# Attention loop of a transformer block on eight cores: a TensorE wait after each group of 512 queries is placed three score tiles later

## The reference

```python
def attn(inputs, Wq, Wk, Wv, Wo, rel_emb):
    q, k, v = (split_heads(inputs @ W) for W in (Wq, Wk, Wv))
    position_bias = compute_bias(rel_emb, qlen, qlen)      # by buckets of key position - query position
    scores = jnp.einsum('bnqd,bnkd->bnqk', q, k) + position_bias
    attn = jax.nn.softmax(scores, axis=-1)
    hidden = jnp.einsum('bnqk,bnkd->bnqd', attn, v)
    return merge_heads(hidden) @ Wo

x = x + attn(layernorm(x), Wq, Wk, Wv, Wo, rel_emb)
x = x + ffn(layernorm(x), w1, w2)      # two linear layers with quantised inputs and weights, GELU between
```

## Time and profile before

| | us |
|---|---|
| median of 2 runs | 9241.44 (9235.77 to 9247.11) |
| the profiled execution's own time | 9240.33 |
| its span on the slowest core (core 5) | 9238.8 |
| spans of the other cores | 9213.0 to 9233.7 |
| TensorE busy, core 5 | 3234.0 (35%) |
| ScalarE busy, core 5 | 2029.9 (22%) |
| VectorE busy, core 5 | 2173.7 (24%) |

### The profile page before, as it was taken

The page is one execution under the profiler, slowest core; times in us unless marked ns, Lnnn a source line. Parts: engine busy times, 40 slices in busy tenths (PEclk is TensorE's granted clock), DMA queues, the critical chain, the costliest instruction groups (busy, mean ns, idle before and its releaser), DMA issues.

```text
span 9238.8 us, 47072 instructions; the slowest of 8 cores (9213.0 to 9238.8 us)
## 1 busy us (share of the span) xinstructions
PE 3234.0 (35%) x12444; PEld 1099.6 (12%) x12444; DVE 2173.7 (24%) x2480; ACT 2029.9 (22%) x2214; POOL 85.1 (1%) x164
## 2 busy tenths in 40 slices
PE   0000015667665100133225235676774000233155
PEld 0000001222121000011112011221221000111022
DVE  0334310000000156266600200000001265366400
ACT  0010102545443000022200003454551000122100
POOL 0000000000000000000000000000000000000000
PEclk9999997888787555566667667887886555666577
DMA  3323222000001310200032122000002401200122
GB/s 69 117 94 115 75 59 50 14 27 14 16 25 47 113 40 29 60 23 23 26 89 73 62 54 41 23 14 19 23 14 65 116 27 39 47 23 23 50 76 74
DMA packets 661832, 459.49 MB, mean 50 GB/s; under 512 B 546242, under 2 KB 579140, under 8 KB 653380
## 3 DMA queue, kind: packets, MB, share of 16 engines
q1 hardware_dynamic: 652868, 447.81, 16.9%
q0 software_dynamic: 8704, 8.66, 0.7%
HBM read 209.23 MB, written 143.79 MB: 38 GB/s over the span
## 4 chain that ended last, share of the span: by engine, by line
DMA 21%; PE 20%; DVE 19%; ACT 15%; SPq 12%; issue 7%; DVEq 5%; ACTq 2%; PEldq 0%; PEld 0%; POOL 0%; POOLq 0%
SPq L103 9%; ACT AR L718 6%; PE PS L967 5%; DMA ARF<-w_in 4%; DVEq L276 3%; PE PS L656 3%; DVE qst_b L290 3%; PE PS L699 2%; PE PS L707 2%; DVE qst_u L298 2%; DVE qst_c L285 2%; SPq L106 2%; PE PS L711 2%; ACT qst_t L930 2%; DVE AR L312 2%
## 5 line engine op out<-in xcount | busy, mean ns | idle before, releaser
L893 PE MATMUL PS<-AR 128*128 128x512 bf16 x2016 | 509.4, 420 | 2427.8 <-DMA AR<-xq_dram 1555.0
L718 ACT ACTIVATE AR<-PS,neg40c 128x1024 bf16<-128x1024 f32 x1024 | 1140.2, 1113 | 485.1 <-PE PS L711 310.6
L967 PE MATMUL PS<-AR 128*128 128x512 bf16 x1984 | 458.8, 391 | 725.7 <-DMA AR<-hq_dram 665.0
L766 DVE RECIPROCAL ARF<-ARF 128x32 f32<-128x32 f32 x16 | 5.7, 353 | 2894.7 <-DMA ARF<-ARF 2894.7
L893 PEld LDWEIGHTS PS<-AR 128*128 128x128 bf16 x2016 | 211.3, 106 | 2726.1 <-issue 2535.6
L699 PE MATMUL PS<-AR 64*128 64x512 bf16 x1024 | 435.9, 426 | 246.5 <-ACTq L92 124.3
L604 PE MATMUL PS<-AR 128*128 128x512 bf16 x448 | 135.7, 454 | 973.3 <-DMA AR<-wv_bf 908.4
L707 PE MATMUL PS<-AR,j_sb 128*128 128x512 bf16 x1024 | 439.8, 429 | 0.0
L703 PE MATMUL PS<-AR 64*128 64x512 bf16 x1024 | 437.0, 427 | 0.0
L711 PE MATMUL PS<-AR,j_sb 128*128 128x512 bf16 x1024 | 434.3, 424 | 0.0
L727 PE MATMUL PS<-AR 128*65 128x512 bf16 x1024 | 400.2, 391 | 90.8 <-ACTq L92 90.8
(11 more groups left out here) (111 smaller groups left out, 3552.4 us busy)
## 6 DMA issues: line engine op xcount, KB each, us to landing
ARF<-w_in SPq DMA_DIRECT2D x64, 512.0 KB
ARF<-w_in SPq DMA_DIRECT2D x32, 1024.0 KB
xtile<-x_in SPq DMA_DIRECT2D x64, 512.0 KB
hq_dram<-AR SPq DMA_DIRECT2D x32, 1024.0 KB
AR<-g_dram SPq DMA_DIRECT2D x32, 992.0 KB
x_dram<-x1t SPq DMA_DIRECT2D x32, 512.0 KB
xtile<-x_dram SPq DMA_DIRECT2D x32, 512.0 KB
xtile<-x_dram SPq DMA_DIRECT2D x64, 256.0 KB
```

The source lines that it names most:

```text
L718: E("scalar", lambda S, ewg=ewg, j=j: S.activation(out=ewg[:, 0:1024], in_=PS[:, 1024 * j:1024 * (j + 1)], func=AF.Exp, bias=neg40c[:], sc ...
L893: E("tensor", lambda T, tt=tt, dc=dc, hg=hg: T.matmul(ps[hg], xqT[dc][:, 128 * tt:128 * (tt + 1)], w1qT[dc][:, 512 * hg:512 * (hg + 1)], s ...
L967: T.matmul(ps[bk], hqT[hc][:, 128 * ttl:128 * (ttl + 1)], w2qT[hc][:, 512 * dg:512 * (dg + 1)], start=(hc == 0), stop=False))
```

## The change

TensorE no longer waits for the four copies directly behind the last PV matmul of a group. The count is kept in `pv_guard`, and TensorE waits for it in the next group of the same pair, ahead of the first PV matmul (`pkt == 0`, which is at `kt == 2`), which writes banks 6 and 7 anew. `pv_guard` is set to None at the start of each pair, so the wait behind a pair's fourth group falls away. POOL's wait is unchanged. Nothing that is computed changes.

```diff
@@ -679,6 +679,7 @@
                 sc_hist = {}
                 vv_hist = {}
                 pv_hist = {}
+                pv_guard = None
                 dminus_, dplus_ = _sat_range()
@@ -723,6 +724,8 @@
                         if kt >= 2:
                             pkt = kt - 2
                             ewp = ew[pkt % 3]
+                            if pkt == 0 and pv_guard is not None:
+                                r.wait("tensor", "S", pv_guard)
                             r.wait("tensor", "S", sc_hist[(qg, pkt)])
                             E("tensor", lambda T, hp=hp, pkt=pkt, ewp=ewp: T.matmul(
                                 PS[0:65, 3072:3584],
@@ -749,7 +752,7 @@
                     sc_hist[(qg, NT - 1)] = sc
                     sc_hist[(qg, NT - 2)] = sc
                     sc_hist[(qg, NT - 3)] = sc
-                    r.wait("tensor", "S", sc)
+                    pv_guard = sc
                     r.wait("gpsimd", "S", sc)
                     if qg == 0:
                         r.wait("gpsimd", "V", r.val("V"))
```

## The result

The changed kernel takes 9143.73 us (median of 7 runs, 9126.8 to 9158.54), the kernel before in the same comparison 9239.14 (6 runs, 9235.73 to 9253.45). The ratio is 0.9892, with a 95% interval from 0.988 to 0.9904: 1.1% less, thus within the 2% that was counted as no change, and clear of the noise. The forecast was 9138 us.

A forecast was written before the change was run, and what follows sets the result against it. No one engine bounds the whole kernel; ScalarE bounds the attention loop at 2.4 GHz. 78 + 30 - 5 = 103 us against 9240.3 gave 9137, and 9138 for the median; range 9108 to 9186.

The forecast's parts named there:

- First term: At 48 group boundaries the first exponential starts at 1576.35, not 1577.98: 1.63 us each, 78 us gained.
- Second term: Behind the boundaries the clock stays at 2.4 GHz and 30 us of exponentials' slips go; bounds -5 to +30 us.
- Third term: Projection groups between pairs: shifted starts make two or three stretches longer, 5 us lost, bounds 24 us to either side.
- What was put at nothing: New wait ahead of the first PV matmul, dropped wait at 16 pair ends, copies beside matmuls: no effect each.
- Signs: In the trace: idle time before exponentials falls from 503 to about 395 us, attention clock slices rise by nearly one.
- A: Clock falls at the boundary as before: gain about 68 to 73 us, time 9170; chance 0.18.
- B: Clock falls later, inside the group, after the 1.4 us hole: 2.4 us late per boundary, time 9253; chance 0.03.

## Why the prediction was right

The forecast was 9138, measured 9143.73; the gain was 95 us where the sum said 103. The slowest cores' spans, 96.6 us apart, show it by terms: 78 + 28 - 13, and 3.7 less in other stages, which the sum didn't have.

*First term, 78 us.* Right: the idle time ahead of the first exponential fell from 87.8 us for 48 boundaries to 9.8 in the mean over cores, 78.0 less. It ends at 0.20 and not at 0.25 us, which is nothing. The run with one early tile shows that the term needs only one tile.

*Second term, 30 us, with the clock.* Right in kind and size. The slips fell from 34 to 8 us (26 less in the mean over cores, 28 on the slowest ones), and the clock fell at none of the 48 boundaries, where it had fallen at all 48. The hole is 1.32 us (forecast 1.4), and TensorE is busy for 2.53 of 3.30 us (forecast 2.3). The run with useless matmuls shows that the cause is TensorE's work in the hole, since nothing else was changed there; the runs with one and two tiles show that the amount counts: with 1.05 of 3.30 us busy the clock fell every time, with 1.67 of 3.40 at three boundaries of four, with 2.5 of 3.30 at none. The Trainium skill says that small idle spells between matmul groups can be enough to bring the clock down ("TensorE: Matmul & The Clock Gate", "A second HAM failure mode: psum-queue depth-cycling"). By that rule only the first term, 78 us, would have come. The trace of the changed kernel doesn't agree: holes of 0.78, 0.77 and 1.32 us in a row left the clock at 1.00. The runs with one tile and with the pipelined order and ScalarE's copy agree in most of their boundaries, with holes of 1.74 and 2.50 us.

*Third term, 5 us lost in the projections.* The mean over the cores is 4.7 us lost between the pairs, of it 3.8 in the projections. The longer projections are those in which the clock was at 0.50 for longer. Before, 89 of the 112 took 22.6 us (3.9 of them at 0.50) and 23 took 24.4 (7.9 at 0.50); after, 80 took 22.6, 21 took 24.3, and 11 took 25.9 (12.6 at 0.50), more than the long length of 24.3 that the prediction had. On the two slowest cores 12.7 us are lost (1256 us in the 14 pieces of core 5 before, 1269 on core 3 after, 1245 on the best core after), and of these only 3 lie in the projections: 7.4 are a longer wait for the bias tables behind them, which the prediction took as fixed. Why the tables come later is not shown. These 12.7 in place of 5 are most of the 8 us between sum and measurement.

*What was put at nothing.* The wait ahead of the first PV matmul cost nothing: at the first boundary the copies ended at 1574.97 and exponential 0, for which the same matmul waits, at 1576.28. The pair ends brought nothing (0.9997). The copies stayed at 0.58 us beside matmuls.

*Signs.* The idle time before the exponentials fell to 405.9 and not to 395, since core 3 waits longer for the bias tables. The clock line was to rise by nearly one in each slice of the attention stages; only three slices did, and the granted clock of the whole span went from 0.737 to 0.751.

*Rivals.* A did not occur. B did not occur here, but its mechanism is real: it appears with one early tile (slips of 0.8 us at a boundary, more than the 0.6 of before) and in full with the pipelined order and ScalarE's copy. I had put 2.4 us late, and written that it decides from 2.25 us of slip per boundary on; there two steps behind the copy took 1.39 and 0.35 us too long, 1.7 at that boundary. So even there B's price was too high.

## What to carry to other kernels

When TensorE waits for an engine that still has copies to make, look for work that needs only what is already free: here the score tiles' own banks were free, and only the PV banks were not, so the wait belonged ahead of the first writer of those banks. Price such a hole twice, as late work and as a possible fall of the clock for the work behind it, and check where that work stands: where the clock fell, it cost 0.3 us with three tiles in hand (one ScalarE copy), 1.0 with one early tile, and 1.7 when the next tile stood behind the wait itself (pipelined order with ScalarE's copy). Once the hole was closed, the copies on the bounding engine were the next cost, one for one: one wide copy in place of four narrow ones gave nearly as much (81 us) as the change itself.

## What was not expected

The stages ahead of the attention loop took 1539 to 1559 us up to the first exponential in most programs, but 1557 to 1568 with the useless matmuls and 1594 to 1628 in the three programs in which VectorE makes the copy out of PSUM, though their code up to there is the same and their DMAs move the same bytes (447.8 MB on the hardware queue over the whole span). SyncE's waits for the weight loads, 0 to 1100 us, core 3, of the changed kernel:

```profile
SPq L120 <- DMA ARF<-w_in: 359.3, 96, 6.0
```

and of the version with VectorE's copy:

```profile
SPq L120 <- DMA ARF<-w_in: 396.2, 95, 6.4
```

Each load waits for the one before it, so 0.4 us on each add up to 37 of the 70 us by which the first exponential of this core is later; in one stretch the loads came every 4.2 us in place of 3.4. The waits for other loads of that stage are longer too. It is not the place of the DRAM tensors as far as one shift of 16 MB tells, and it doesn't come with VectorE's copies within SBUF, which the version with one ScalarE copy has too, with the usual start. What it is stays open. The lesson for a comparison: 50 us of a result can lie in a stage that the edit doesn't touch, and a version is judged by its stage in the trace as well as by its total.

One copy of 65 x 1024 out of two banks took ScalarE 1.01 us, and two of 64 x 512 took 1.16; VectorE needed 1.22 us for the same 65 x 1024.
